# Scratch rows in natural order and taps turned on chip, in a two-pass mixing and convolution kernel

## What is computed

```python
def reference(x, cond, length, weights, log_dt, C, log_A_real, A_imag, D):
    u = x + einsum('bct,bcd->bdt', x, weights[cond])       # weights: 16 matrices of 128x128
    dt = exp(log_dt); A = -exp(log_A_real) + 1j * A_imag   # 128 channels x 64 modes
    dtA = A * dt[:, None]
    Ct = (C[..., 0] + 1j * C[..., 1]) * (exp(dtA) - 1.0) / A
    K = 2.0 * einsum('hn,hnl->hl', Ct, exp(dtA[:, :, None] * arange(2048))).real
    y = causal_convolution(u, K) + u * D[:, None]          # by FFT, first 2048 outputs
    return u + y * (arange(2048) < length[:, None])[:, None, :]
```

## Time and profile before

| | |
|---|---|
| median of three runs | 1077.04 us |
| span of the profiled execution, first to last instruction | 1073.5 us |
| execution time nearest to that span | 1073.87 us |
| granted TensorE clock, mean | 0.990 |
| PE busy | 94% of the span |
| DVE / ACT / POOL busy | 67% / 54% / 61% |
| moved by DMA | 305.0 MB |

### The profile page before, as it was taken

The page is one execution under the profiler, slowest core; times in us unless marked ns, Lnnn a source line. Parts: engine busy times, 40 slices in busy tenths (PEclk is TensorE's granted clock), DMA queues, the critical chain, the costliest instruction groups (busy, mean ns, idle before and its releaser), DMA issues.

```text
span 1073.5 us, 30051 instructions
## 1 busy us (share of the span) xinstructions
PE 1004.2 (94%) x11612; PEld 741.1 (69%) x11612; DVE 717.1 (67%) x1647; ACT 580.4 (54%) x1230; POOL 654.8 (61%) x1377
## 2 busy tenths in 40 slices
PE   7977779778999999999999999999999999999998
PEld 4333234233347887888888888888888888888886
DVE  3988950000006877788788788778778778888875
ACT  2643444344535555566566556556655656656654
POOL 3211051201207887888888888888888888888740
PEclk9999999899999999999999999999999999999999
DMA  8999999999989999999999999999999999999994
GB/s 323 424 421 424 423 422 423 363 424 424 424 314 326 292 281 261 252 230 229 232 225 234 223 233 235 224 234 222 230 224 225 226 212 250 224 223 229 237 220 124
DMA packets 169630, 305.01 MB, mean 284 GB/s; under 512 B 78274, under 2 KB 111426, under 8 KB 161298
## 3 DMA queue, kind: packets, MB, share of 16 engines
q1 hardware_dynamic: 169170, 302.64, 98.5%
q0 software_dynamic: 160, 0.20, 0.1%
q10 hardware_dynamic: 160, 0.26, 0.1%
HBM read 152.37 MB, written 134.41 MB: 267 GB/s over the span
## 4 chain that ended last, share of the span: by engine, by line
PE 77%; DMA 17%; ACT 3%; issue 2%; DVE 0%; SPq 0%; ACTq 0%
PE bank L603 16%; DMA u_scratch<-stage 15%; PE bank L617 15%; PE bank L570 14%; PE bank L556 11%; PE bank L544 9%; PE bank L582 7%; PE bank L609 5%; ACT stage L743 2%; DMA x_f<-in_x 1%; DMA gt_sb<-g_sb 0%; ACT ring L743 0%; DMA u_row<-u_scratch 0%; DMA u_scratch<-ring 0%; DVE st_sb L1039 0%
## 5 line engine op out<-in xcount | busy, mean ns | idle before, releaser
L603 PE MATMUL bank<-toep,u_t 128*128 128x192 f16 (+1 forms) x3072 | 342.5, 220 | 0.2
L617 PE MATMUL bank<-g_sb,st_sb 128*128 128x256 f16 x1536 | 306.0, 273 | 0.8 <-issue 0.8
L544 PE MATMUL bank<-x_f,w_buf 128*128 128x512 f32 x512 | 243.0, 621 | 52.1 <-ACT stage L743 29.0
L556 PE MATMUL bank<-ident,u_row 128*128 128x128 f32 x1024 | 277.5, 275 | 4.4 <-DMA u_row<-u_scratch 1.7
L773 ACT ACTIVATE st_sb<-bank 128x128 f16<-128x128 f32 x448 | 123.8, 276 | 256.3 <-PE bank L582 194.1
L603 PEld LDWEIGHTS bank<-toep,u_t 128*128 128x128 f16 x3072 | 231.4, 99 | 13.7
L544 PEld LDWEIGHTS bank<-x_f,w_buf 128*128 128x128 f32 x512 | 95.9, 196 | 190.3 <-issue 116.7
L1057 DVE COPY_PREDICATED o_sb<-mask,u_row 128x512 f32<-128x512 uint8 x256 | 212.5, 830 | 16.6 <-issue 16.5
L1034 DVE SCALAR_TENSOR_TENSOR u_t<-bank,u_t 128x512 f16<-128x512 f32 x256 | 176.1, 688 | 56.0 <-ACT u_t L757 56.0
L1039 DVE TENSOR_TENSOR st_sb<-bank,st_sb 128x128 f16<-128x128 f32 x448 | 130.4, 291 | 88.3 <-ACT st_sb L773 83.2
L609 PE MATMUL bank<-toep,x_t 128*128 128x64 f16 x2048 | 188.2, 193 | 0.2 <-issue 0.2
(11 more groups left out here) (135 smaller groups left out, 969.5 us busy)
## 6 DMA issues: line engine op xcount, KB each, us to landing
x_f<-in_x SPq DMA_DIRECT2D x64, 1024.0 KB, 19.6
u_row<-u_scratch SPq DMA_DIRECT2D x128, 512.0 KB, 5.9
out<-o_sb SPq DMA_DIRECT2D x254, 256.0 KB, 3.8
u_scratch<-stage SPq DMA_DIRECT2D x48, 1024.0 KB, 17.7
toep<-k_scratch SPq DMA_DIRECT2D x64, 256.0 KB, 6.1
u_scratch<-ring SPq DMA_DIRECT2D x14, 512.0 KB, 14.6
u_scratch<-kept SPq DMA_DIRECT2D x12, 448.0 KB, 6.5
gt_sb<-g_sb SPq DMA_TRANSPOSE x124, 5.4
```

What stands on the lines that cost most here:

```text
L544: last = pe.matmul(bank[:, 4 * (n % 2) + k, :], w_buf[n % XS][:, :], x_f[n % XS][:, k * 512:(k + 1) * 512], start=True, stop=True)
L556: last = pe.transpose(bank[:, 4 + q, g * P:(g + 1) * P], u_row[c % 4][:, h, g, tb * P:(tb + 1) * P], ident[:, :])
L603: pe.matmul(bank[:, y, col + tb * P + NM:col + Q], u[:, h, tb, a, rows_], t[:, h, b, NM:Q - tb * P], start=first, stop=False, skip_group_c ...
L617: last = pe.matmul(bank[:, y, col:col + Q], st[:, h, a, gr * ROWS:(gr + 1) * ROWS], g[:, h, b, :], start=False, stop=(m == 2), skip_group_ ...
```

## The change

Three edits.

1. **Inputs of the tables loaded once.** Three of the six `nat` loads go. After the weights of batch 0, GpSimd waits for the other three and copies them into the second column halves; TensorE's transposes wait for the copies.
2. **Taps turned on chip.** The pieces are kept as float32 (`k_taps`); a sixth step at batch 35 transposes them by 16 small TensorE transposes into [channel, 256], ScalarE and VectorE split them into high and low part in `k_rows`, and one GpSimd DMA stores a row of 1536 bytes per channel in place of the five DMAs.
3. **u's scratch in natural order**, [channel][batch][2048]. The first 48 batches are stored in runs of 8 KB. A channel's u rows are loaded by two DMAs of 64 partitions, rows of 4 KB with a step of 8 KB, in place of one DMA of 128.

```diff
-PIECES = 5
+PIECES = 6
...
-    u_dram = nc.dram_tensor("u_scratch", [H, ROWS, NG, Q], F32, kind="Internal")
+    u_dram = nc.dram_tensor("u_scratch", [H, NB, T], F32, kind="Internal")
...
             def store_u(n, s):
-                dst = bass.AP(u_dram, n * NG * Q, [[ROWS * NG * Q, H], [NB * NG * Q, JJ], [1, NG * Q]])
-                sp.dma_start(dst, stage[n % STAGES][:, :, :, :].rearrange("p j a t -> p j (a t)")).then_inc(s, 16)
+                sp.dma_start(u_dram[:, n, :], stage[n % STAGES][:, :, :, :].rearrange("p j a t -> p (j a t)")).then_inc(s, 16)
...
-            sp.dma_start(nat[0][:, NM:P], log_a[:, :]).then_inc(s_in[0], 16)
-            sp.dma_start(nat[1][:, NM:P], a_im[:, :]).then_inc(s_in[0], 16)
-            sp.dma_start(nat[2][:, P:2 * P], c_in.rearrange("h n c -> h (n c)")).then_inc(s_in[0], 16)
...
             def load_u(i, c, h):
                 wait(sp, s_ov, 4 * (UN * i + c - 4) + 2 * h + 2)
-                sp.dma_start(u_row[c % 4][:, h, :, :].rearrange("p g q -> p (g q)"),
-                             bass.AP(u_dram, (2 * (UN * i + c) + h) * (ROWS * NG * Q), [[NG * Q, ROWS], [1, NG * Q]]))\
-                    .then_inc(s_row[c % 4][h], 16)
+                for j in range(JJ):
+                    sp.dma_start(u_row[c % 4][j * NB:(j + 1) * NB, h, :, :].rearrange("p g q -> p (g q)"),
+                                 u_dram[2 * (UN * i + c) + h, :, j * NG * Q:(j + 1) * NG * Q]).then_inc(s_row[c % 4][h], 16)
...
-            sp.wait_ge(s_kd, 80)
+            sp.wait_ge(s_kd, 16)
...
                 weights(n)
+                if n == 0:
+
+                    pool.wait_ge(s_in[0], 48)
+                    for k, columns in enumerate((NM, NM, P)):
+                        pool.tensor_copy(nat[k][:, columns:2 * columns], nat[k][:, 0:columns]).then_inc(s_nat, 1)
...
-                    for k in range(2):
-                        pool.wait_ge(s_kl, 2 * k + 2)
-                        for part in range(2):
-                            dst = bass.AP(k_dram, (2 * HT * k + part) * KROW + P, [[16, 16], [2 * KROW, HT], [1, 16]])
-                            pool.dma_start(dst, k_body[k][:, part, :, :]).then_inc(s_kd, 16)
-                    pool.wait_ge(s_kl, PIECES)
-                    pool.dma_start(k_dram.ap()[:, :, 0:P], k_head[:, :, :]).then_inc(s_kd, 16)
+                    pool.wait_ge(s_kl, 2)
+                    pool.dma_start(k_dram.ap().rearrange("h a t -> h (a t)"),
+                                   k_rows[:, :, :].rearrange("p a t -> p (a t)")).then_inc(s_kd, 16)
...
+                    pe.wait_ge(s_kh, PIECES - 2)
+                    for z in range(16):
+                        last = pe.transpose(bank[:, b, z * 16:(z + 1) * 16], ap(k_taps, z, [[16, H]], 16), ident[0:16, 0:16])
...
+                    act.activation(ap(k_rows, P, [[16, 16], [1, 16]]), ap(bank, b * 512, [[1, 16], [16, 16]]), ACT.Copy)\
+                        .then_inc(s_kh, 1)
...
-            for piece in range(PIECES - 1):
-                dve.wait_ge(s_kh, piece + 1)
...
+            tt(ap(k_rows, KROW + P, [[16, 16], [1, 16]]),
+               ap(bank, 4 * ((TAPS + PIECES - 1) % 2) * 512, [[1, 16], [16, 16]]),
+               ap(k_rows, P, [[16, 16], [1, 16]]), SUB)
```

More of the change, by code:

```diff
@@ L154, in build @@
         quarter_turn = sb("quarter_turn", [P, 1], F32, shaping)
-        ai, cr, ci, dec, e_re, omega, cycles, freq = (
-            sb(n, [P, H], F32, shaping) for n in ("ai", "cr", "ci", "dec", "e_re", "omega", "cycles", "freq"))
+        natural = ExitStack()
+        ai, cr, ci = (sb(n, [P, H], F32, natural) for n in ("ai", "cr", "ci"))
+        natural.close()
+        k_rows = sb("k_rows", [P, 2, KROW], F16, shaping)
+        dec, e_re, omega, cycles, freq = (
+            sb(n, [P, H], F32, shaping) for n in ("dec", "e_re", "omega", "cycles", "freq"))
         s_re, s_im, k_a, k_b, c_top = (sb(n, [P, H], F32, shaping) for n in ("s_re", "s_im", "k_a", "k_b", "c_top"))
         k_zero = sb("k_zero", [P, 1], F32, shaping)
-        k_head = sb("k_head", [P, 2, P], F16, shaping)
-        k_body = [sb(f"k_body{k}", [16, 2, HT, 16], F16, shaping) for k in range(2)]
+        k_taps = sb("k_taps", [16, H, 16], F32, shaping)
         shaping.close()
@@ L171, in build @@
         outs.close()
-        sb("shaping_bytes", [P, H * 16 + 256 + NS + 1 + 13 * H + 1 + P + 2 * HT * 16], F32)
+        sb("shaping_bytes", [P, H * 16 + 256 + NS + 1 + 13 * H + 1 + H * 16], F32)
         bank = ctx.enter_context(nc.psum_tensor("bank", [P, 8, 512], F32))
@@ L179, in build @@
         s_turn, s_wave, s_abs = (sem(n) for n in ("s_turn", "s_wave", "s_abs"))
-        s_tab, s_msk, s_zero = (sem(n) for n in ("s_tab", "s_msk", "s_zero"))
+        s_tab, s_msk, s_zero, s_nat = (sem(n) for n in ("s_tab", "s_msk", "s_zero", "s_nat"))
         s_km, s_kh, s_kl, s_kd = (sem(n) for n in ("s_km", "s_kh", "s_kl", "s_kd"))
@@ L269, in store_u @@
             def store_u(n, s):
-                dst = bass.AP(u_dram, n * NG * Q, [[ROWS * NG * Q, H], [NB * NG * Q, JJ], [1, NG * Q]])
-                sp.dma_start(dst, stage[n % STAGES][:, :, :, :].rearrange("p j a t -> p j (a t)")).then_inc(s, 16)
+                sp.dma_start(u_dram[:, n, :], stage[n % STAGES][:, :, :, :].rearrange("p j a t -> p (j a t)")).then_inc(s, 16)
             def store_half(n, j, first, last, s):
-                dst = bass.AP(u_dram, (first * ROWS + j * NB + n) * NG * Q, [[ROWS * NG * Q, last - first], [1, NG * Q]])
-                sp.dma_start(dst, half_buffer(n, j)[first:last, :, :].rearrange("p a t -> p (a t)")).then_inc(s, 16)
+                sp.dma_start(u_dram[first:last, n, j * NG * Q:(j + 1) * NG * Q], half_buffer(n, j)[first:last, :, :].rearrange("p a t -> p (a t)")).then_inc(s, 16)
             load_x(0)
             sp.dma_start(nat[0][:, 0:NM], log_a[:, :]).then_inc(s_in[0], 16)
-            sp.dma_start(nat[0][:, NM:P], log_a[:, :]).then_inc(s_in[0], 16)
             sp.dma_start(nat[1][:, 0:NM], a_im[:, :]).then_inc(s_in[0], 16)
-            sp.dma_start(nat[1][:, NM:P], a_im[:, :]).then_inc(s_in[0], 16)
             sp.dma_start(nat[2][:, 0:P], c_in.rearrange("h n c -> h (n c)")).then_inc(s_in[0], 16)
-            sp.dma_start(nat[2][:, P:2 * P], c_in.rearrange("h n c -> h (n c)")).then_inc(s_in[0], 16)
             sp.dma_start(logs[:, 0, :], log_dt.partition_broadcast(P)).then_inc(s_in[1], 16)
@@ L500, in taps @@
                     pe.wait_ge(s_tab, 1)
-                if piece < PIECES - 1:
+                if piece < PIECES - 2:
                     for h in range(32):
@@ L504, in taps, with taps_read @@
                                          b_re[:, 32 * piece + h, :], start=True, stop=True)
-                else:
-                    last = pe.matmul(bank[:, b, 0:1], c_top[:, :], b_re[:, 0, 0:1], start=True, stop=True)
+                elif piece == PIECES - 2:
+                    last = pe.matmul(bank[:, b, 0:1], c_top[:, :], b_re[:, 0, 0:1], start=True, stop=True)
+                else:
+                    pe.wait_ge(s_kh, PIECES - 2)
+                    for z in range(16):
+                        last = pe.transpose(bank[:, b, z * 16:(z + 1) * 16], ap(k_taps, z, [[16, H]], 16), ident[0:16, 0:16])
                 last.then_inc(s_km, 1)
+            def taps_read(piece):
+                if piece < PIECES - 2:
+                    pe.wait_ge(s_kh, piece + 1)
+                else:
+                    pe.wait_ge(s_kl, piece - PIECES + 3)
             def turned(piece, b):
@@ L523, in _ @@
                 if n == 1:
-                    pe.wait_ge(s_in[0], 96)
+                    pe.wait_ge(s_nat, 3)
                     srcs = [nat[0][:, 0:P], nat[1][:, 0:P],
@@ L540, in _ @@
                     if k == 0 and 0 <= piece < PIECES:
-                        pe.wait_ge(s_kl, piece + 1)
+                        taps_read(piece)
                     if k == 0 and 0 <= turn < 4:
@@ L551, in transpose_u @@
                 if k % 8 == 0:
-                    pe.wait_ge(s_row[c % 4][k // 8], 16 * (i + c // 4 + 1))
+                    pe.wait_ge(s_row[c % 4][k // 8], 32 * (i + c // 4 + 1))
                 if g == 0:
@@ L700, in taps_hi @@
                 act.wait_ge(s_km, piece + 1)
-                half = slice(32 * (piece % 2), 32 * (piece % 2) + 32)
-                act.activation(k_body[piece // 2][:, 0, half, :].rearrange("p h a -> p (h a)"),
-                               bank[0:16, b, :], ACT.Copy).then_inc(s_kh, 1)
+                if piece < PIECES - 2:
+                    act.activation(k_taps[:, 32 * piece:32 * piece + 32, :].rearrange("p h a -> p (h a)"),
+                                   bank[0:16, b, :], ACT.Copy).then_inc(s_kh, 1)
+                elif piece == PIECES - 1:
+                    act.activation(ap(k_rows, P, [[16, 16], [1, 16]]), ap(bank, b * 512, [[1, 16], [16, 16]]), ACT.Copy)\
+                        .then_inc(s_kh, 1)
             def g_hi(i, c):
@@ L712, in _ @@
             for n in range(NB):
```

(16 more changed lines are left out.)

## The result

The changed kernel took 1083.05 us (median), the kernel before 1075.59 us (median of all its runs beside it); the ratio is 1.0075, with a 95% interval of 1.0052 to 1.0098. One of its six executions took 2053.13 us, nearly twice as long at a full clock; it is left out of the ratio, its cause is not known, and the other five have a median of 1082.65 us. The changed kernel is slower, by some 8 us. The time lies in the stated range and on the wrong side: the forecast was 0.4% faster, with 0.24 for slower. The profiled execution took 1080.32 us, with a span of 1078.2 against 1073.5.

What follows compares the result with a forecast made beforehand. DMA was taken to bound the first pass until about 271 us and PE the second; -0.7 - 3.5 - 3.4 + 1.3 + 1.5 = -4.8 us, from 1077.04 to 1072.2 us, range 1066 to 1089.

Steps and rivals of the forecast that it cites:

- What bounds what: Whole kernel: DMA bounds the first pass until about 271 us, so savings there count; PE paces the second pass.
- Edit 1: Start of the kernel: three of seven small loads, run at 114 GB/s, go; -0.7 us, bounds 0 and -1.1.
- Edit 2: First pass, taps DMAs: 3.9 us of DMA time lost at 298 GB/s, 0.4 left; -3.5 us, added transposes free.
- Edit 3a: First-pass stores: 8 KB packets replace pairs of 4 KB, 0.07 us saved per store, 48 stores; -3.4 us, bounds 0 and -5.3.
- Edit 3b (i): Between the passes: the first u load needs both halves and one more issue; +1.3 us, bounds 0 and +2.5.
- Edit 3b (ii): Second-pass slots: later landings still in time, SyncE's +0.9 us a slot covered by 3.0 us of waiting; no cost.
- Edit 3b (iii): Second-pass DMA throughput: 2.1 us more work per slot, charged 0.03 us x 62; +1.5 us, bounds 0 and +16.6.
- A: Second-pass slots: halves fill the DMA queue and PE waits, 0.27 us in each of 62 slots, 1087.3 us; chance 0.17.
- the dip: First pass near 195 us: the drop to 298 GB/s after GpSimd's taps DMAs was to vanish.
- the rate: First pass, 44 to 186 us: DMA was to rise from 423 to about 429 GB/s.
- the first load: Start of the second pass: the first pass was to end some 7 us earlier.
- PE's wait for u rows: Second pass: PE's wait for u rows or turned tables was to stay near zero.

Runs made afterwards that it cites:

- e2: The kernel before with each channel's u rows loaded by two DMAs of 64 partitions from contiguous HBM, against the kernel before: 1.0077, 8.3 us slower.
- e4: The kernel before with u's scratch stored in 8 KB runs, read back by one contiguous 128-partition DMA per channel (outputs differ), against the kernel before: 0.9995.
- e5: The kernel before with halved loads for channel pairs 0 to 3 alone, of 64, against the kernel before: 1.0057, 6.1 us slower.
- e6: The kernel before with halved loads for channel pairs 12 to 63 alone, against the kernel before: 0.9968.
- e9: The kernel before with all channels of the last 16 batches stored in the first pass, one seventh of late stores left, against the kernel before: 1.0159.
- e3: The kernel before with each channel's u rows loaded by two DMAs of 128 partitions, rows of 2 KB, against the kernel before: 1.0035, 3.8 us slower.
- e10: As e9, with only one seventh of the late stores left, plus loads by halves for all pairs, against the kernel before: 1.0149.
- e11: The kernel before with edit 2 alone (taps turned on chip), against the kernel before: 0.9959, 4.4 us faster.
- e7: The changed kernel run once more, all three edits, against the kernel before: 1.0060.
- e1: The kernel before with edits 1 and 2, scratch layout, stores and loads of u as before, against the kernel before: 1068.96 us, 0.9959.
- e12: The kernel before with edit 1 alone (three small loads fewer, three copies on GpSimd), against the kernel before: 0.9982.

## Why the prediction was wrong, step by step

**What bounds what**: right. Time saved on DMA before 271 us came through to the first load: -4.7 us in the changed kernel.

**Edit 1**, -0.7: within what was measured (-0.2%, with zero in the interval), but the row it was worked out from does not carry it. The 114 GB/s of 10 to 12 us are not the small loads' price: with all six loads in place the same window moved 221 to 345 GB/s in e2, e4, e5, e6 and e9 and 108 to 203 in e3, e10 and e11, and with three of them gone 265 to 304. The copies took 0.64 us for all three, and the weights behind them were done by 12.5 us, as the working had it.

**Edit 2**, -3.5: right; e11 gave -4.4, with an interval of -7.1 to -1.7. The added transposes took 1.9 us at batch 35, where 2.4 were counted, and nothing waited for them that showed.

**Edit 3a**, -3.4: too large; e4 measured -0.5, with an interval of -2.7 to +1.6. The packets did change as read: from 61 to 181 us,

```profile
DMA packets 7310, 51.07 MB, mean 426 GB/s; under 512 B 1081, under 2 KB 1081, under 8 KB 1081
q1 hardware_dynamic: 7302, 50.97, 100.9%
```

no packet of 4 KB is left. The step that failed is the one from packet time to batch time. By the earlier trace rows's way of working, an 8 KB packet takes (1.009 x 120 x 16 - 15) / 6229 = 0.309 us, so the pair's 0.010 us is saved as predicted. But only half of it became rate, 423 to 426 GB/s or 0.7% (over the stretch to 271 us an estimate of 1.7 us); the other half went into a share that fell from 101.6 to 100.9%. Why the share falls stays open. Batches do not resolve so little: stage stores 9 to 33 took 120.5 us in the changed kernel, 118.6 in e7 and 119.9 in e4, and 117.8 to 120.2 in the kernels with 4 KB runs.

**Edit 3b (i)**, between the passes, +1.3: mis-sized. It costs 2.0 us to slot 0 and 2.0 more to slot 1 (in the other kernels with halves among the late stores 2.3 to 3.1 to slot 0). The step took the first load's chain alone. It left out that SyncE issues 12 loads in place of 6 before the work of slot 1, 6.9 us of issuing in place of 3.0, and that these issues become the chain.

**Edit 3b (ii)**, the slots' latencies and SyncE's time: right in that nothing waits for them. Landings stayed at 5.5 us, and e6 shows no cost for 104 channels. SyncE's added time was undersized: two halves took 2 x 0.87 us for 0.74, some 2.0 us a slot where 0.9 were counted; its waits covered that.

**Edit 3b (iii)**, throughput, +1.5, bounds 0 and 16.6: the step that turned the sign. Edits 1 and 2 gave their 4.4 us (e1), and the halves took 8.3 us (e2) where 1.3 + 1.5 = 2.8 were counted. The narrow transfers do cost the DMA more time, for loads as for stores, if less than was taken: 237 to 255 GB/s at a share above 1 where whole loads reach 348, which is 1.4 to 1.5 times the time for the mix, against 1.75 for the loads in the working (2.43 us for 1.39). What failed is the place where it was charged. The late stores from 319 to 392 us served as evidence that the queue has room (11.77 us a slot with 1.6 us of work more); but they had used up that room, and the same slots now had to take the halves on top, by the working's own price 2.1 us each. I charged 62 slots 0.03 us; the runs show nothing in the last 52 of them (e6), and from the first load to slot 12 the kernels with halves among the late stores took 4.3 to 13.5 us longer than before, by one profile each. Also "where the engines work off a backlog, narrow transfers need not cost extra" was wrong: at 315 to 325 us there was a backlog (late stores landed after 10 us and more), and the rate still fell to 255.

The Trainium skill ("SBUF — State Buffer", on the DMA port swizzle) puts 64 partitions at about half the rate. The rate here fell by a third, from 348 to 237, in a mix of halves, tiles and late stores, and e3 shows that the width does it. The rule's direction was right about the transfer, and the rival that I drew from it (A, all slots at 0.27 us, 1087) was still wrong in its mechanism: the loss of 8 us comes from the first slots.

**The numbers.** The range held, but by luck: its upper part was rival A's price for every slot, which is not what happened. Of the signs, the dip went and the steady products stayed 11.6 us apart; the rate rose to 426 and not to 429, the first load came 4.7 us earlier and not 7, and PE's wait for u rows, which was to stay near zero, grew to 6.1 us. The chance of slower was too low: the right question, what the halves cost where the queue is fullest, was answerable from the earlier trace rows and the diff, and was not asked.

**Left open.** Whether edits 1 and 2 lose part of their 4.4 us when the halves are there; the split of e3's 3.8 us; how the loss among the late stores splits between SyncE's issues and the slower transfers.

## What to carry to other kernels

Price a slower transfer where the queue is fullest and something waits for its end, not by the mean of the steady part: 8 channels of 128 alone cost 6.1 us (e5), and 104 others nothing (e6). A stage in which extra transfers went through at no cost shows room that was there, and has none left for yours. Try the parts of a change alone: edit 2 by itself gives the gain (0.9959), edit 1 cannot be told from nothing, and the third undid them.

## What was not expected of the hardware

**PE's granted clock at the first batch differed between executions.** In the kernel before, PE stood idle for 3.05 us ahead of the first product, and the granted clock was 0.50 (1.2 GHz) from 12 to 14 us; the eight matmuls of batch 0 took 5.40 us. In the changed kernel it was idle for 1.93 us, the clock stayed at 1.00 (2.4 GHz), and they took 3.70:

```profile
10.84 3.70 PE L554 MATMUL bank<-x_f,w_buf 128*128 128x512 f32 x8 [1.93 <-DMA x_f<-in_x]
```

The same holds in the experiments, with 5.40 us after 3.41 us of idleness (e3) and 3.70 us after 1.60 to 2.66 us (e1, e2, e4 to e12), whether edit 1 was in or not. So most of the 1.9 us by which the first stage store came earlier is this, and not the missing loads; it hardly lasts. e2, e5 and e6, which start like the changed kernel, reach the first load at 315.0 to 315.7 us, and before and e3, which start late, at 316.1.

**A DMA of 64 partitions took SyncE longer to issue than one of 128**, with the same row length. Of the loads between the passes the first took 0.46 to 0.50 us in all kernels with halves and the next three 0.59 to 0.60 each; with whole rows the first took 0.32 to 0.34 us, the second 0.43, and the third and fourth 0.43 to 0.56.
